# Both rounds of score products ahead of the transposes of the pair before

## The reference

```python
Q = split(q @ wq + bq); K = split(k @ wk + bk); V = split(v @ wv + bv)   # 16 heads, in the last layer 8
scores = einsum('bhqd,bhkd->bhqk', Q, K) / sqrt(DK)
scores = where(mask == 0, -big, scores)                                  # not in the last layer
A = softmax(scores, axis=-1)
out = einsum('bhqk,bhkd->bhqd', A, V) ... @ wo + bo                      # then residual and norm
```

## Time and profile before

| | us |
|---|---|
| median of 3 runs | 726.18 (725.76 to 728.63) |
| the profiled execution | 727.51 |
| its span | 725.6 |
| PE busy | 659.6 (91%) |
| PEld busy | 468.9 (65%) |
| DVE busy | 509.8 (70%) |
| ACT busy | 455.5 (63%) |
| POOL busy | 319.8 (44%) |
| score products L569, 1536 instructions | 123.8 |
| transposes L606, 704 instructions | 119.7 |

### The profile page before, as it was taken

One profiled execution on the slowest core, in us unless ns is written; L12 is line 12 of the kernel. 1 busy time (PEld: TensorE's weight loads), 2 busy tenths in 40 slices (PEclk: granted clock), 3 DMA queues, 4 the chain that ended last, 5 costly groups with the idle time before them and its releaser, 6 DMA issues.

```text
span 725.6 us, 26905 instructions
## 1 busy us (share of the span) xinstructions
PE 659.6 (91%) x9470; PEld 468.9 (65%) x9470; DVE 509.8 (70%) x1259; ACT 455.5 (63%) x1274; POOL 319.8 (44%) x540
## 2 busy tenths in 40 slices
PE   1999999999999999999999779899946989999995
PEld 1566666777777766666666537899933656666773
DVE  0598999888887778888888633344413689988784
ACT  1467677777777787777777442355513567777874
POOL 2244544466667653333477661245532254543110
PEclk9999999999999999999999669999975899999998
DMA  8333434332333321111111001122232011111110
GB/s 265 92 100 91 95 94 95 75 71 66 97 90 112 89 69 34 44 36 42 37 53 39 25 32 45 31 65 68 64 108 70 23 35 43 35 29 33 48 41 27
DMA packets 60047, 47.32 MB, mean 65 GB/s; under 512 B 7833, under 2 KB 54429, under 8 KB 58800
## 3 DMA queue, kind: packets, MB, share of 16 engines
q1 hardware_dynamic: 53152, 28.57, 14.2%
q10 hardware_dynamic: 4528, 13.25, 7.4%
q0 software_dynamic: 2272, 4.24, 1.8%
HBM read 25.41 MB, written 14.79 MB: 55 GB/s over the span
## 4 chain that ended last, share of the span: by engine, by line
PE 68%; issue 15%; POOL 7%; DVE 4%; ACT 2%; DMA 2%; ACTq 1%; SPq 0%; POOLq 0%; DVEq 0%
PE ps L569 11%; PE ps L606 9%; PE ps L792 5%; PE ps L730 5%; PE ps L803 5%; PE ps L655 4%; PE ps L643 4%; PE ps L672 4%; PE ps L738 4%; POOL k_by_j L499 3%; PE ps L711 3%; PE ps L758 2%; PE ps L656 2%; PE ps L591 2%; PE ps L683 2%
## 5 line engine op out<-in xcount | busy, mean ns | idle before, releaser
L1098 DVE TENSOR_REDUCE top<-ps 128x16 f32<-128x1024 f32 (+1 forms) x96 | 108.9, 1134 | 38.7 <-PE ps L569 37.0
L499 POOL TENSOR_TENSOR k_by_j<-k_t,cst 128x512 f32<-128x512 f32 (+1 forms) x96 | 95.6, 996 | 81.4 <-ACT k_t L907 45.0
L491 POOL TENSOR_TENSOR rstd<-spread,half_neg 128x1 f32<-128x1 f32 x80 | 44.6, 557 | 193.2 <-DVE spread L1191 115.0
L569 PE MATMUL ps<-k_by_j,q_t 32*64 32x256 f32 (+1 forms) x1536 | 123.8, 392 | 1.2
L606 PE MATMUL ps<-cst,prob 128*128 128x128 f32 x704 | 119.7, 291 | 1.7 <-ACT prob L928 1.5
L606 PEld LDWEIGHTS ps<-cst,prob 128*128 128x128 f32 x704 | 76.8, 143 | 61.5 <-issue 45.2
L1057 DVE RECIPROCAL inv<-ps 128x128 f32<-128x128 f32 x96 | 91.8, 956 | 32.9 <-PE ps L738 30.6
L928 ACT ACTIVATE prob<-prob 128x1024 f32<-128x1024 f32 (+1 forms) x96 | 94.8, 988 | 22.8 <-DVE prob L1114 22.5
L1114 DVE TENSOR_TENSOR prob<-ps,top 128x1024 f32<-128x1024 f32 (+1 forms) x96 | 108.3, 1128 | 0.7
L877 ACT ACTIVATE prob_t<-ps 128x512 f32<-128x512 f32 (+1 forms) x96 | 53.9, 561 | 38.0 <-PE ps L606 37.5
L865 ACT ACTIVATE prob_t<-ps 128x512 f32<-128x512 f32 (+1 forms) x96 | 53.9, 561 | 28.5 <-PE ps L606 27.4
(11 more groups left out here) (155 smaller groups left out, 1213.4 us busy)
## 6 DMA issues: line engine op xcount, KB each, us to landing
sorted_rows<-zero_rows ACTq DMA_DIRECT2D x32, 276.2 KB, 2.7
stage_m<-in_m SPq DMA_DIRECT2D x80, 64.0 KB, 2.0
stage_x<-x_t SPq DMA_DIRECT2D x80, 64.0 KB, 1.9
mow<-in_mow SPq DMA_DIRECT2D x18, 256.0 KB, 3.1
stage_kv<-in_ctx_t SPq DMA_DIRECT2D x64, 64.0 KB
rows_in<-sorted_rows SPq DMA_DIRECT2D x39, 65.0 KB, 1.8
wat<-in_wat ACTq DMA_DIRECT2D x1, 1280.0 KB, 7.6
stage_x<-in_x_t SPq DMA_DIRECT2D x16, 64.0 KB, 2.0
```

The lines of the kernel that those rows point to most:

```text
L499: pool.tensor_tensor(k_by_j[:, p, 0:nj, :], k_t[:, p:p + 1, :].broadcast_to([128, nj, TOK]), cst[:, cj:cj + nj].unsqueeze(2).broadcast_to( ...
L569: mm = pe.matmul(ps[S * b:S * b + S, 2 * p + bank, r * nj * S:(r + 1) * nj * S].rearrange("p (h k) -> p h k", k=S), q_t[rows_g, p, S * b:S ...
L1098: dve.tensor_reduce(top[:, p, 0:nh].rearrange("p (b h) -> p b h", b=2), sc, AX.X, ALU.max).then_inc(top_d, 1)
```

## The change

Round 1 of the scores is issued directly behind round 0, ahead of the feed-forward product and of all transposes. Its two former places are removed. The first four transposes of the pair at offset 3 then follow both rounds, and the last four follow them at once. No instruction, wait or buffer is added or taken away; on the matrix engine the order changes, on the other engines nothing. Round 1 keeps its wait for the end of round 0.

```diff
@@ -583,6 +583,7 @@
                     wait_pair(pe, q_e, pr)
                     wait_pair(pe, kj_d, pr)
                     score_round(pr, 0).then_inc(round_d, 1)
+                    score_round(pr, 1).then_inc(score_d, 1)
 
                 pr = follows(at, OFF_FY, FF)
                 if pr is not None:
@@ -606,9 +607,6 @@
                             mm = pe.transpose(ps[:, 2 * p + half, k * 128:(k + 1) * 128],
                                               prob[:, p, q * 128:(q + 1) * 128], ident)
                         mm.then_inc(done, 1)
-                        scored = at(OFF_SCORE)
-                        if half == 0 and scored is not None:
-                            score_round(scored, 1).then_inc(score_d, 1)
 
                 pr = at(OFF_XT)
                 if pr is not None:
@@ -655,10 +653,6 @@
                     pe.matmul(ps[:, B_PROJ, 0:128], wat[:, ph, 0, :], stage_x[:, p, :], start=True, stop=True)
                     pe.matmul(ps[:, B_PROJ, 128:256], wat[:, ph, 1, :], stage_kv[:, p, :], start=True, stop=True)\
                         .then_inc(proj_d, 1)
-                pr = at(OFF_SCORE)
-                if pr is not None and at(OFF_PV) is None:
-                    score_round(pr, 1).then_inc(score_d, 1)
-
                 pr = at(OFF_OUT)
                 if pr is not None:
                     wait_pair(pe, heads_d, pr)
```

## The result

The changed kernel takes 730.67 us (median of 4, 730.07 to 731.59) where the kernel before takes 726.55 (median of 4, 725.76 to 728.63): ratio 1.0053, interval 1.0029 to 1.0077. It is slower, by 4.1 us (0.53%) where 7.9 were forecast. The profiled execution took 730.49 with a span of 728.6, 3.0 more than before.

What follows compares the result with a forecast made beforehand. The matrix engine's stream plus its stalls was taken as the bound, ScalarE's queue setting the slot. Terms 6.0 + 9.1 + 0.5 − 3.5 − 4.2 = +7.9 on 726.18 gave 734.1 us, range 727.5 to 741.

Steps and rivals of the forecast that it cites:

- The length of the stream up to XT: Matrix engine, round 0 to XT: unchanged at 2.26 us, two saved changes of shape paying for the newly exposed wait.
- the exposed wait: Matrix engine: round 1's wait for round 0's end, formerly hidden under transposes, makes round 1 start 0.74 us behind round 0.
- Rival B: Faster: round 1 streams behind round 0 at the lower bound, 0.21 us less than taken; 721.5 us, chance 0.08.
- L617 waits for xn_f: Feed-forward slots: the transpose of xn_f waits behind late copy 0, slots near 8.0 instead of 7.4; 14 slots, +9.1 us.
- The two slots of L619 alone: Slots with L619 but no FY: xn_f bound by GpSimd now and by copy 0 after; estimate +0.5 us.
- the routing slots: Phase 3 with routing: earlier scores remove VectorE's idle time before the maxima; 10 slots x 0.35, −3.5 us.
- the 1 us of the forecast: Start of group one: earlier exponential ends the first transposes' wait; less the exposed wait −1.0, first value products about 1 us earlier.
- Phase 5: Last phase: half the heads, shorter rounds and x_t well before OUT, so 0.
- The plain slots: Phases 0 to 4: copy 1, x_t and OUT come 0.13 us later in ScalarE's queue; 46 slots, +6.0 us.
- The starts of the groups: First slots of both groups: scores come earlier and waits shrink, together −4.2 us, bounds −1 and −6.
- no change: Whole kernel: a difference under 0.5% (3.6 us) is called no change; chance of same 0.15.
- Rival C: No change: copy 0's delay is absorbed in the plain slots, so the +6.0 goes; 728.1 us, chance 0.15.

Runs made afterwards that it cites:

- e6: Changed kernel, but in feed-forward slots round 1 stands behind the feed-forward product FY; 732.28 us against 729.34 for the kernel before, ratio 1.0044.
- e1: Changed kernel, but in the 16 slots with L619 round 1 goes back between the transpose sets; 723.06 us against 728.5 for the kernel before, ratio 0.9928.
- e3: Changed kernel with xn_f moved ahead of copy 0 on ScalarE; 728.33 us against 728.5 for the kernel before, ratio 0.9995.
- e9: Changed kernel measured again, unaltered, beside the kernel before on the same chip; 731.49 us against 726.78, ratio 1.0056.
- e7: Kernel before, rounds interleaved, with only x_t moved ahead of copy 1 in slots without L619; 720.67 us against 729.34, ratio 0.9899.
- e2: Kernel before with round 1 directly behind round 0 only in each group's first scoring slot; 725.44 us against 728.5, ratio 0.9962.
- e8: Changed kernel, but 16 L619 slots keep interleaved rounds and x_t precedes copy 1 in all others; 710.45 us against 729.34, ratio 0.9754.
- e4: Changed kernel with x_t moved ahead of copy 1 in slots without L619; 719.64 us against 728.5 for the kernel before, ratio 0.9879.

## Why the prediction was right

*The steps that held.* R1 starts 0.75 behind R0 (0.74 forecast from one self-wait of the masks). The length of the stream up to XT is unchanged, 2.27: the two changes of shape that are saved pay for the exposed wait and no more, and e6 shows the same trade from the other side. The Trainium skill's page "TensorEngine Tiling (Array Packing)", section Key Properties, says that a change of the tiling mode drains the engine; the traces agree that it costs time, 0.06 to 0.10 each here. Rival B is out. L617 waits for xn_f (0.69) with slots of 8.01, forecast 8.04; e1 and e3 show that it is this and that it comes through ScalarE. The two slots of L619 alone gave +0.52, the routing slots −0.39 each. In group two the first slot is 1.43 shorter (forecast 1.5) and the third 0.43 (0.4 forecast for each of three, the other two gave 0.13 and 0.15). In e9, where the clock rises late as in the kernel before, the first value products come 12.7 after the first R0 instead of 13.7: the 1 us of the forecast. Phase 5 gave 0.2 where 0 was forecast.

*The terms that were mis-sized.* The plain slots, forecast 46 x 0.13 = 6.0, gave 1.81 + 1.52 + 1.04 = 4.4 over 45 slots. In written-out slots it was 0.12, but in every other slot of the hardware loops 0.05, as in those slots copy 0 starts 0.70 behind T0 instead of 0.76 and everything behind it 0.07 earlier; I had read one slot and multiplied. The starts of the groups gave −2.3 and −2.6 where −4.2 was forecast; of the first, 1.3 is the varying rise of the clock (e9).

*What I did not foresee.* −0.96 ahead of the first scores, where no instruction changed: this stretch ran from 18.3 to 20.1 in the twelve profiles and is chance. −1.80 in the end of group one and the experts, where −0.3 was forecast. Nearly all of it (−1.73) lies between R0 of the last pair of group one and the last gate product, the drain of the pipeline, and there the matrix engine's granted clock differs. Each row gives the stretch, its length, the busy times of PE, PEld, DVE, ACT and POOL, then the granted clock, and last the transfers. In order: the kernel before, the changed kernel, and e7, which has the old order of the rounds:

```profile
401.30:424.42 23.12, 13.54 (x162) 10.86 (x158) 13.45 (x79) 8.90 (x26) 14.30 (x30) 0.59 0.08 25
```

```profile
406.96:428.35 21.39, 10.31 (x162) 8.07 (x158) 13.39 (x80) 8.67 (x26) 14.35 (x31) 0.74 0.09 30
```

```profile
396.16:417.86 21.70, 10.53 (x162) 8.05 (x158) 13.92 (x79) 8.79 (x26) 14.31 (x30) 0.74 0.08 26
```

The part above on the time before names only the half-speed stretch from 536 to 568 us, but in that profile the clock also stood at half from 405.6 to 429.5, from 4.3 us into the drain on. In the changed kernel it fell 10.4 into the drain (at 417.4), in e7 10.2, in the other profiles with the new order 8.6 to 11.8; these drains take 21.1 to 21.9 whatever the order of the rounds. In e2 it fell 3 us ahead of the drain, which took 24.17. So most of the −1.8 goes with the moment at which the clock fell, and the earlier scores of the last slots give about 0.4 (e8 21.26 against e7 21.70), no more than the spread of these profiles.

*What the number is worth.* Errors that cancel did not make it: the slots gave +10.0 where +12.3 was forecast, the two starts −4.9 for −4.2, and nearly every other term came out below its forecast too. Three places that differ between executions or go with the clock, the time before the first scores (−1.0), the rise of the clock (−1.3, part of the starts) and its fall (about −1.4), took some 3.7 off the difference of the spans. The forecast was clear of "no change" by its own line, 3.6 us, but the result was so by little: 4.1 in the medians (4.7 in e9) and 3.0 in the spans (4.2 in e9). Its side of the line is in part luck; that the change costs time is not, as both intervals lie above 1. Rival C is out all the same, as the plain slots did get longer. The timed difference of 4.1 is larger than that of the spans by 1.1, within the spread of the single times.

The clock bears on the timed ratios too. The timed executions of the kernel before, where the record has their clock, were granted 0.950 to 0.961 over the span, those of the changed kernel (e9 included) 0.960 to 0.966. On the chip of e1 to e4 the eight executions of the kernel before at 0.958 or more have a median of 727.2, the twelve at 0.956 or less 729.1, all twenty 728.5. I estimate from these that the ratios there would be higher by up to 0.2% at the same granted clock; on the chip of e9 the same working gives nothing.

*What had been overlooked.* The forecast named copy 1 and x_t as the stall of every plain slot and priced 0.13 of it. That the same stall was there before the change, and that mending it is worth 8.7 us with the old order (e7) and 12.7 with the new (e4 against the changed kernel), was not asked, though it stood in the same rows: OUT follows x_t by 0.14 in the earlier trace rows, and XT was done 0.4 before x_t began.

*Open.* Why ScalarE picks up copy 0 0.06 sooner in every other loop slot. Whether the order of the rounds moves the moment at which the clock falls behind group one, or chance does: the early falls are in two of the three profiles with the old order and in none of the nine with the new, but e7 has the old order and the late fall. A kernel without the wait between the rounds was not tried, because the rounds write the same banks.

## What to carry to other kernels

When work is moved ahead of a producer on one in-order engine, price what stands behind that producer's consumer in the consumer's own queue: here a copy that came 0.74 us later cost 8.6 us in 14 slots, through the small activation queued behind it. If an edit shifts when results come, fit the consumers' order to it: the same change is a loss of 0.5% with ScalarE's old order and, with x_t ahead of the second copy and the old order kept in 16 slots, part of a gain of 2.5% (1.4% of it by the order of the rounds, e8 against e7). Count a per-slot effect in a written-out slot and in both slots of a loop's turn before multiplying.

## What the runs showed of the hardware

A score round directly behind another that it waits for starts 0.74 to 0.75 after it in the full-speed slots of phases 0 to 4 (0.54 in phase 5 with its half-length rounds, 1.22 at half speed), 0.16 later than a full-shape successor without a wait (0.59). A score round behind full-shape products starts 0.10 later than transposes would there (1.09 in e6 against 0.99), and transposes behind score rounds lose 0.06 on their first (0.66 against 0.60 for four).

The matrix engine's products can run at half speed (2.35 for two rounds instead of 1.41) while the granted clock of that stretch reads 1.00 in the profile: it did so in both kernels before 25 us. When they reach full speed differs between two executions of the changed kernel by about 7 us (about 25.5 us, or between 31.3 and 32.8), with the same work ahead of it. In the profile of the kernel before half speed lasts beyond 30 us, and not only to 28.

At the end of group one the granted clock fell from full to half in all twelve profiles, at a moment between 3 us before and 11.8 us after R0 of the last pair; the drain took 24.17 in the first case (e2) and 21.11 in the last (e4).
